# D times xs scaled in place by GpSimd and added over four states, with the projection tiles of a unit begun three steps sooner

## The reference

```
xs, z = split(h @ in_w);  xs = silu(xs)
proj = xs @ xproj_w
dt = softplus(proj[..., :512] + dt_bias);  Bm, Cm = the next 64 and 64 columns
hst = hst * exp(dt_t * A) + (dt_t * x_t) * B_t        # for each t, 512 channels x 64 states
y_t = sum over the states of hst * C_t
y = ys + xs * Dskip
return y * silu(z) @ out_w
```

## Time and profile before

| what | us |
|---|---|
| median of 3 runs | 3308.93 (3303.74 to 4097.8) |
| profiled execution | 3303.74 |
| its span, first to last instruction | 3301.9 |
| mean granted TensorE clock | 0.989 |
| unit 4, first DVE scan | 1308.50 |

### The profile page before, as it was taken

The page is one execution under the profiler, slowest core; times in us unless marked ns, Lnnn a source line. Parts: engine busy times, 40 slices in busy tenths (PEclk is TensorE's granted clock), DMA queues, the critical chain, the costliest instruction groups (busy, mean ns, idle before and its releaser), DMA issues.

```text
span 3301.9 us, 59343 instructions
## 1 busy us (share of the span) xinstructions
PE 3203.5 (97%) x22634; PEld 2506.2 (76%) x22634; DVE 2873.1 (87%) x2843; ACT 2817.0 (85%) x4644; POOL 2318.9 (70%) x1105
## 2 busy tenths in 40 slices
PE   8999999999999999999999999999999979999899
PEld 4888898999999989999998999899888432222244
DVE  3999999999999999999999999999999378888121
ACT  6999999999999999999999999999987335777620
POOL 1889999999999999999999999998888000000000
PEclk8999999999999999999999999999999988999999
DMA  3223222222222222222222222222211034422000
GB/s 120 68 85 82 76 72 74 67 71 69 72 71 90 73 71 73 71 75 67 77 73 68 71 68 73 72 73 67 83 64 60 0 77 84 82 39 33 15 7 19
DMA packets 199901, 218.82 MB, mean 66 GB/s; under 512 B 80033, under 2 KB 149665, under 8 KB 199361
## 3 DMA queue, kind: packets, MB, share of 16 engines
q1 hardware_dynamic: 199618, 215.02, 23.1%
HBM read 194.29 MB, written 18.19 MB: 64 GB/s over the span
## 4 chain that ended last, share of the span: by engine, by line
PE 73%; ACT 17%; DVE 6%; issue 3%; DMA 1%; SPq 0%; POOL 0%; DVEq 0%; ACTq 0%
PE psum L1621 20%; PE psum L1389 16%; PE psum L1615 15%; PE psum L1612 11%; ACT arena L1072 7%; ACT arena L1054 6%; PE psum L1699 4%; PE psum L1688 3%; PE psum L1672 3%; DVE arena L1299 2%; DVE row_max L1342 2%; PE psum L1641 1%; ACT arena L1096 1%; ACT arena L1057 0%; PE psum L1483 0%
## 5 line engine op out<-in xcount | busy, mean ns | idle before, releaser
L1299 DVE TENSOR_TENSOR_SCAN arena<-arena,psum 128x512 f32<-128x512 f32 x2048 | 2373.3, 1228 | 57.0 <-PE psum L1615 43.9
L774 POOL TENSOR_TENSOR arena<-arena 128x1024 f32<-128x1024 f32 x1024 | 2226.3, 2187 | 256.5 <-DVE arena L1299 233.0
L1072 ACT ACTIVATE arena<-arena,a_neg 128x512 f32<-128x512 f32 x2048 | 1440.8, 723 | 43.6 <-PE psum L1615 43.0
L1621 PE MATMUL psum<-ident,arena 128*128 128x128 f32 x8192 | 1230.4, 273 | 1.7 <-POOL arena L774 1.7
L1054 ACT ACTIVATE arena<-arena,bT 128x512 f32<-128x512 f32 x1536 | 1109.3, 722 | 0.0
L1615 PE MATMUL psum<-ident,arena 128*128 128x128 f32 x6144 | 1008.7, 273 | 0.0
L1621 PEld LDWEIGHTS psum<-ident,arena 128*128 128x128 f32 x8192 | 961.5, 141 | 2.1 <-POOL arena L774 2.1
L1612 PE MATMUL psum<-arena 128*128 128x128 f32 x4096 | 820.7, 282 | 32.1 <-ACT arena L1054 16.5
L1612 PEld LDWEIGHTS psum<-arena 128*128 128x128 f32 x4096 | 647.4, 191 | 246.7 <-issue 151.1
L1615 PEld LDWEIGHTS psum<-ident,arena 128*128 128x128 f32 x6144 | 743.6, 142 | 0.0
L1389 PE MATMUL psum<-arena 128*128 128x512 f32 (+1 forms) x1440 | 673.2, 589 | 8.4 <-DVE arena L1171 2.9
(11 more groups left out here) (117 smaller groups left out, 886.0 us busy)
## 6 DMA issues: line engine op xcount, KB each, us to landing
arena<-bc_dram SPq DMA_DIRECT2D x256, 512.0 KB, 3.7
arena<-diag_dram SPq DMA_DIRECT2D x224, 128.0 KB, 2.1
arena<-qk_dram SPq DMA_DIRECT2D x96, 128.0 KB
diag_dram<-arena SPq DMA_DIRECT2D x32, 256.0 KB, 4.4
qk_dram<-arena SPq DMA_DIRECT2D x12, 512.0 KB, 4.9
arena<-in_x SPq DMA_DIRECT2D x4, 512.0 KB, 10.3
arena<-skip_w SPq DMA_DIRECT2D x64, 32.0 KB, 2.0
arena<-sums_dram SPq DMA_DIRECT2D x64, 32.0 KB, 1.8
```

The costliest lines, as they stand in the source:

```text
L774: pool.tensor_tensor(out[:, :, way], h_now[:, :, way], c_row, ALU.mult)\
L1072: act.activation(decay[:, w % AHEAD, f], dt_[:, u % 2, f], ACT.Exp, scale=a_neg[:, d, f, st:st + 1])\
L1299: dve.tensor_tensor_scan(hs[:, w % RING, f, rows][:, way], decay[:, w % AHEAD, f, way], psum[:, 4 + n % U_BANKS, way], end_state(w - DS, f ...
L1621: return pe.matmul(psum[:, c, f * P:(f + 1) * P], hs[:, w % RING, f, at:at + P], ident[:, :], is_transpose=True, start=False, stop=w % DS ...
```

## The change

- `skip_w` and the ACT copies that made it go. `attn_sb`, which shared its place, gets a buffer of its own.
- `scale_skip`: POOL multiplies xs by D in place, in four calls of 128x512 for each unit: for unit 0 before the steps begin, for the others in steps 48, 50, 60 and 62 of the unit before, once dt * xs is made and the dt tiles are done with xs.
- `turn_skip`: PE turns the scaled xs into the sums as it turns the products, four turns in each of the first four states (steps 2 to 5), where before there were 16 ordinary matmuls in step 2. The first turn of a product now starts the sum.
- In units 1 to 6 the projection tiles begin at step 1, not 4, in the order zs, xs, yT, not xs, yT, zs. All other places stay.

```diff
+SKIP_STEPS = (48, 50, 60, 62)
...
-        skip_w = sb("skip_w", [P, 2, NI, P])
-        attn_sb = skip_w.rearrange("p a b c -> p a (b c)")
+        attn_sb = sb("attn_sb", [P, 2, HALF])
...
-                place([step for k in range(NI) for step in (xs_[k], yT_[k], zs_[k])], 4)
+                place([step for k in range(NI) for step in (zs_[k], xs_[k], yT_[k])], 1)
...
+            def scale_skip(u, f):
+                pool.tensor_scalar(xs[:, f], xs[:, f], d_skip[:, unit(u)[0], f:f + 1], None, ALU.mult).then_inc(s["skip_ready"], 1)
+
+            pool.wait_ge(s["ssm_small_in"], 80)
+            pool.wait_ge(s["tile_full"], first["bc", 0] + 1)
+            pool.wait_ge(s["dtx_ready"], NI)
+            for f in range(NI):
+                scale_skip(0, f)
...
+                    if st in SKIP_STEPS and u < UNITS - 1:
+                        f = SKIP_STEPS.index(st)
+                        pool.wait_ge(s["dtx_ready"], NI * (u + 1) + f + 1)
+                        pool.wait_ge(s["tile_full"], first["dt", u + 1, NI - 1] + 1)
+                        scale_skip(u + 1, f)
...
-            def skip_weights():
-                for d in range(2):
-                    for f in range(NI):
-                        act.activation(skip_w[:, d, f], ident[:, :], ACT.Copy, scale=d_skip[:, d, f:f + 1])\
-                           .then_inc(s["skip_w_ready"], 1)
...
-                                 is_transpose=True, start=False, stop=w % DS == DS - 1 and f == NI - 1)
+                                 is_transpose=True, start=w % DS == 0 and f == 0, stop=w % DS == DS - 1 and f == NI - 1)
+
+            def turn_skip(u, f, c):
+                if c == 0:
+                    pe.wait_ge(s["skip_ready"], NI * u + f + 1)
+                pe.matmul(psum[:, c, f * P:(f + 1) * P], xs[:, f, c * P:(c + 1) * P], ident[:, :],
+                          is_transpose=True, start=False, stop=False)
 
             def reduce_state(w, f):
+                st = w % DS
+                if f == 0 and st < NI:
+                    for c in range(TB):
+                        turn_skip(w // DS, st, c)
...
                 if c == 0:
-                    pe.wait_ge(s["skip_w_ready"], 2 * NI)
                     pe.wait_ge(s["prod_done"], 2 * (w + 1))
                 for f in range(NI):
-                    pe.matmul(psum[:, c, f * P:(f + 1) * P], xs[:, f, c * P:(c + 1) * P],
-                              skip_w[:, unit(u)[0], f], start=f == 0, stop=False)
-                for f in range(NI):
                     o = turn_h(w, f, c)
+                turn_skip(u, 0, c)
```

More of the change, by code:

```diff
@@ L201, in build @@
             centred squared rstd_step rstd_ready normed h_ready
-            exp_step dt_ready dtx_ready skip_w_ready bc_rows_ready a_exp a_ready silu_ready
+            exp_step dt_ready dtx_ready skip_ready bc_rows_ready a_exp a_ready silu_ready
             dve_const uT_ready u_full decay_ready scan_done prod_done reduce_done gated
@@ L961, in do @@
                         act.activation(a_neg[:, :, :, :], a_neg[:, :, :, :], ACT.Exp).then_inc(s["a_exp"], 1)
-                        skip_weights()
                     if kind == "up":
```

## The result

The changed kernel takes 3318.23 us (median of 20 runs, 3312.89 to 3320.26), the one before 3305.98 beside it. The ratio is 1.0033, 95% interval 1.0026 to 1.0040: slower by about 11 us, clear of its interval and far under 2%. The range held it. The forecast, 3310, was low: its sum had the change at +4.4 us, and 11 to 12 were measured.

What follows compares the result with a forecast made beforehand. PE was taken to bound only steps with projection tiles, ACT the long silu's step, DVE elsewhere. Terms +4.05 - 0.3 + 0.6 = +4.4 on 3303.74 gave 3308.1; allowing for the higher median, 3310 us, range 3294 to 3326.

Steps and rivals of the forecast that it cites:

- Four paces: Scan steps: PE 3.95 us without a tile, 4.81 with half; DVE 4.45 in even units; ACT 4.3; POOL 4.28.
- the walk: Step-by-step reckoning through unit 4 of when each engine starts after the change; step 26 comes 0.9 us late.
- The skip matmuls hidden in step 2: In units 1 to 7, PE's burst in step 2 is covered by DVE's gates but for some tenths.
- The tiles three steps sooner: Tiles in steps 1 to 20 delay step 26 by 0.9 us in even units, 0.45 in odd.
- +4.05: Sum in us of the earlier tiles' delays over three even units (2.7) and three odd ones (1.35).
- The gates' 0.65: The half tile in step 1 makes the gates wait 0.65 us later, by the unit 4 reckoning.
- +0.6: POOL's scalings at 0.85 us apiece cost 0.2 us in each of three even units, 0 in odd.
- the point from which POOL decides: Price of one scaling, about 1.3 us, from which POOL's backlog sets the time.
- its own last sign: The forecast is wrong if one POOL scaling costs over 1.3 us.
- rival (b): POOL decides: at 2.19 us a scaling, 22 us in all, 3332; chance 0.13, prices between 1.3 and 2.19 included.
- covered: Scalings in steps 60 and 62 cost nothing, since PE is slower there (4.81) and the gates come.
- rival (c): The clock falls in steps 21 to 24, without 512-column PE products: 83 us at half clock, 3393; chance 0.02.

Runs made afterwards that it cites:

- e7: Changed kernel with scaling as a two-input multiply, projection tiles at their old steps and eight turns each in steps 2 and 3: 3307.49 us, ratio 0.9998 to before.
- e5: Changed kernel with projection tiles at their old steps and POOL scaling only 4 of 512 elements per tile: 3310.30 us, ratio 1.0009 to before.
- e2: Kernel before with only the projection tiles' places moved to start at step 1; old skip matmuls, no POOL scaling: 3311.87 us, ratio 1.0012 to before.
- e3: Changed kernel with POOL scaling only 4 of 512 elements per tile, turns and places kept: 3310.58 us, ratio 1.0010 to before.
- e6: Changed kernel with POOL scaling only 4 of 512 elements and ACT's step-24 silu on one chunk of four: 3305.29 us, ratio 0.9998 to before.
- e4: Changed kernel with the scaling as a two-input multiply, D broadcast as second input: 3311.92 us, ratio 1.0015 to before.

## Why the prediction was right, and what in it was not

The range, the sign and "within 2%" came out; the forecast was 8 us low by the medians.

**What bounds.** Four paces, nearly equal, as told. That PE isn't the bound in step 2 is shown by e7, where its saved work changed nothing. That DVE ends last wherever PE has no tile isn't shown by a run of its own. Of the walk's readings one is a little off: 1415.98 to 1420.39 is 4.41, not 4.3, for ACT's seven; 4.3 is its pace without a wait.

**The skip matmuls hidden in step 2.** Right (e5, e7). The turns in steps 3 to 5 were in the walk, 0.44 each; alone they cost 0.7 a unit, 4.2 in six. The places alone, with the burst, cost 5.8 (e2), and both together, without POOL's scaling, 5.3 (e3). They don't add up; by the starts of the steps both are won back in part in the steps without tiles before the silu, but no run sets that apart.

**The tiles three steps sooner.** The walk gave 0.9 in an even unit and e3 measured 0.99; for the odd ones it gave 0.45, measured 0.78 (0.65 without unit 1). +4.05 was 5.3. The gates' 0.65 was 0.62. In even units ACT's silu is the bound as told (e6). In odd ones ACT is 0.64 late at step 25, not 0.45, and DVE close behind it. There the stretch of steps 3 to 24 is 1.0 to 1.1 longer (0.45 in 3 to 6, the rest to 24), because the turns take PE's lead over DVE at a time when the tiles at 4.81 against DVE's 4.69 don't let it come back; 0.8 to 1.0 of it returns in steps 24 to 31, where the old stall is now under DVE's own lateness. That reading rests on the starts of the steps, and no run sets it apart.

**POOL.** This is the term that was mis-sized, +0.6 where 6.8 was measured. The step that failed is the price: "I take the same fixed part and one input at the memset's slope", 0.85, with the two-input multiply as the upper end. Four elements cost 338 ns in e3 and 512 cost 1581, so some 0.33 fixed and 2.4 ns an element, above the 1.75 of the two-input one, (2187 - 1290) / 512. The slope that I took, 0.88 ns, doesn't follow from the memset's row either, which gives 1889 / 2048 = 0.92 at most. A multiply with one streamed input is not the cheaper one here. The other half of it is borne out: the point from which POOL decides was put at about 1.3 a piece; at 1.10 it costs 1.1 us in six units, at 1.58 6.5, and with unit 7 6.8, between the prediction's 3.5 at 1.29 and its 22 at 2.19. By its own last sign, a scaling over 1.3, the forecast was wrong; the range held because its upper end reached half-way into rival (b). A second step failed with the price: "covered", of the scalings in steps 60 and 62. At 1.58 the gates wait for that backlog, 2.6 of the 6.8 us, and in odd units, put at 0, that is the whole of POOL's share. The value that the Trainium skill's page GPSIMD Engine Reference (3.1 Elementwise) gives for 512 elements, 769 ns, is half of what was measured.

**Unit 0**: -0.3 was -0.1. PE's wait for ACT's eviction grew from 0.94 to 2.49, as told, and took up the first half of the burst; the second half put DVE 1.55 ahead at step 3, and the turns of steps 3 to 5, on top of tiles, took 1.3 of that back, 0.43 in each. **The clock in steps 21 to 24**: no fall, the granted clock of the changed kernel was 1.00 from 166 to 2404 us of its span; rival (c) is out.

**Not foreseen**: 1.25 in unit 7, and 1.3 behind the last scan (14.7 of the span less 13.4). The first goes with TensorE's granted clock in unit 7 and not with an edit, as the last section tells; what the second is stays open.

## What to carry to other kernels

Where three engines run within a few per cent of one another, work is free or dear by its step, not by its engine: ask of each moved piece which engine is late in the step that it leaves and in the step that it enters. A small job on an engine with 30% idle can still set the pace if it stands where that engine's idle time is already spent, and its price must come from its own form of instruction: bound it by more than the nearest dearer-looking one.

## What the runs showed of the hardware

GpSimd's multiply of 128x512 float32 by one scalar for each partition took 1.58 us, the multiply of two such inputs 1.29, and the same with the scalar broadcast as the second input 1.10. The short one of four elements took 0.34.

TensorE's granted clock fell to its lower level (1.2 GHz) for stretches in unit 7 whose number differs from kernel to kernel: two in the profiled executions of the kernel before, e2, e4 and e6, three in those of all the others. The growths of unit 7 in the table part in the same way: -0.5 to 0.1 with two, 0.8 to 1.9 with three. The windows of the kernel before and of e3 over the same 120 us, in which e3 has the lower clock and less done:

```profile
2330.00:2450.00 120.00, 109.82 (x829) 97.47 (x828) 119.05 (x104) 105.12 (x169) 97.46 (x45) 0.97 0.18 61
```

```profile
2330.00:2450.00 120.00, 110.39 (x818) 98.12 (x817) 118.03 (x103) 104.28 (x168) 96.42 (x44) 0.96 0.18 59
```

In e3 the whole 1.25 of unit 7 comes between its steps 31 and 51, where these stretches lie. That accounts for it in size and place, but no run was made to set it apart, and why some executions have a third stretch stays open.
